# A transformer tower on one core: softmax remainders by pairs of units, one rounded exponential less in every sixth pair, value products two steps later

## The reference

```
nb = s // w                                  # 8 blocks of 128 queries
sb = einsum('bhnqd,bhnkd->bhnqk', qb, kb)    # each block sees 3 blocks of keys
probs = softmax(concatenate([sg, sb + bias])) # sg: the score of the global token 0
out = einsum('bhnqk,bhnkd->bhnqd', pb, vb) + einsum('bhsg,bhgd->bhsd', pg, vg)
out = out.at[:, :, g].set(og)                # token 0 attends to everything
```

## Time and profile before

| | |
|---|---|
| median of the runs | 921.63 us |
| profiled execution, its own time | 924.96 us |
| its span, first to last instruction | 923.2 us |
| mean granted TensorE clock | 0.954 of full speed |
| PE, PE weight loads | 805.3 us (87%), 615.1 us (67%) |
| DVE, ACT, POOL busy | 587.9 us, 583.4 us, 555.3 us |
| attention steps, round 1 | about 62 to 155 us of the span |

### The profile page before, as it was taken

How to read it: one execution, slowest core, us unless ns; L and a number is a source line. 1 busy time by engine, 2 the same in 40 slices (tenths; PEclk the granted TensorE clock), 3 DMA queues, 4 the chain that set the end, 5 groups by cost and what they waited for, 6 DMA issues and landing times.

```text
span 923.2 us, 23664 instructions
## 1 busy us (share of the span) xinstructions
PE 805.3 (87%) x8467; PEld 615.1 (67%) x8467; DVE 587.9 (64%) x1897; ACT 583.4 (63%) x1622; POOL 555.3 (60%) x820
## 2 busy tenths in 40 slices
PE   4989998999999989999999899999998977886397
PEld 1767766666777666667776666677765645785397
DVE  3678845447988454568884543798845436898454
ACT  2769985338799853277998534779985213665164
POOL 3548875544478755365887554448875445658345
PEclk9899999999999989999999999999998995999599
DMA  2320000602000006030000060200000613001231
GB/s 64 100 52 3 3 14 10 195 1 81 3 3 4 16 31 195 5 99 18 3 4 14 10 196 0 81 3 4 3 3 1 195 55 151 1 8 47 87 102 34
DMA packets 38597, 43.85 MB, mean 47 GB/s; under 512 B 7163, under 2 KB 33882, under 8 KB 38346
## 3 DMA queue, kind: packets, MB, share of 16 engines
q1 hardware_dynamic: 18348, 19.40, 7.1%
q10 hardware_dynamic: 17860, 18.19, 6.3%
q0 software_dynamic: 2272, 4.74, 1.6%
HBM read 20.70 MB, written 21.59 MB: 46 GB/s over the span
## 4 chain that ended last, share of the span: by engine, by line
PE 60%; DVE 13%; ACT 9%; issue 5%; SPq 5%; POOL 4%; DMA 2%; ACTq 1%; POOLq 0%; DVEq 0%
PE bank L1344 7%; PE bank L1481 6%; PE bank L1505 5%; PE bank L1432 4%; PE bank L1550 4%; PE bank L1551 4%; PE bank L1484 3%; PE bank L1370 3%; ACT p L732 3%; PE bank L1381 3%; PE bank L1435 3%; PE bank L1651 2%; PE bank L1660 2%; SPq L453 2%; DVE p L993 2%
## 5 line engine op out<-in xcount | busy, mean ns | idle before, releaser
L568 POOL TENSOR_TENSOR p<-p 128x384 f16<-128x384 f32 (+1 forms) x320 | 270.8, 859 | 110.2 <-ACT p L732 102.0
L986 DVE TENSOR_REDUCE nmx<-bank 128x1 f32<-128x384 f32 (+1 forms) x384 | 191.0, 512 | 36.4 <-PE bank L1435 32.1
L731 ACT ACTIVATE p<-bank 128x384 f32<-128x384 f32 (+1 forms) x384 | 174.0, 453 | 42.6 <-PE bank L1484 28.9
L732 ACT ACTIVATE p<-bank 128x384 f16<-128x384 f32 (+1 forms) x384 | 174.0, 453 | 0.0
L1481 PE MATMUL bank<-stack 103*128 103x128 bf16 x1056 | 145.1, 222 | 4.4 <-DMA stack<-mtr 3.1
L1484 PE MATMUL bank<-bandb,idb 128*128 128x128 bf16 x672 | 135.3, 222 | 0.0
L1432 PE MATMUL bank<-stack 100*128 100x384 bf16 (+1 forms) x384 | 120.3, 313 | 1.6 <-DVE nmx L986 1.3
L1505 PE MATMUL bank<-vst,p 128*128 128x49 bf16 x2112 | 115.5, 185 | 1.7 <-POOL p L568 1.7
L1481 PEld LDWEIGHTS bank<-stack 103*128 103x128 bf16 x1056 | 88.2, 98 | 28.9 <-issue 15.6
L1435 PE MATMUL bank<-bandb,idb 128*128 128x128 bf16 x672 | 100.9, 219 | 0.0
L1505 PEld LDWEIGHTS bank<-vst,p 128*128 128x128 f16 x2112 | 91.7, 97 | 11.6 <-POOL p L568 2.1
(11 more groups left out here) (252 smaller groups left out, 1799.7 us busy)
## 6 DMA issues: line engine op xcount, KB each, us to landing
xs<-zrow ACTq DMA_DIRECT2D x8, 2193.0 KB, 11.8
xt<-xs SPq DMA_DIRECT2D x23, 129.0 KB, 2.1
w2s<-in_w SPq DMA_DIRECT2D x4, 576.0 KB
mwbs<-in_mwb SPq DMA_DIRECT2D x1, 2064.0 KB, 9.1
mw2s<-in_mw SPq DMA_DIRECT2D x1, 2048.0 KB, 13.4
lnrow<-in_lnr SPq DMA_DIRECT2D x4, 480.0 KB
stack<-mtr SPq DMA_DIRECT2D x96, 3.0 KB
w1b<-in_w SPq DMA_DIRECT2D x4, 291.0 KB
```

The lines of the kernel that those rows point to most:

```text
L568: nc.gpsimd.tensor_tensor(p2[:, u % RING, 0:w], p32[:, u % RING, 0:w], p1[:, u % RING, 0:w], ALU.subtract).then_inc(p2_pool, 1)
L731: nc.scalar.activation(p32[:, s % RING, 0:w], ps[2 + s % 3][:, 0:w], ACT.Exp).then_inc(p32_ready, 1)
L732: nc.scalar.activation(p1[:, s % RING, 0:w], ps[2 + s % 3][:, 0:w], ACT.Exp).then_inc(p1_ready, 1)
L986: nc.vector.tensor_reduce(nmx[:, vn % 3, h:h + 1], nat_bank(v)[:, 0:w], AX.X, ALU.max, negate=True).then_inc(max_done, 1)
```

## The change

Five edits, all in the attention steps:

1. POOL forms remainders for two units in one instruction (128 x 768 at the inner blocks, 128 x 512 at the edge blocks), at every second step, once both units' exponentials are done.
2. In every sixth pair (units 10 and 11 of each 12) ACT writes only the 32-bit exponential. POOL rounds both units to 16 bits with one copy, and DVE forms the two remainders, one unit a step, at step u + 4 instead of u + 1.
3. `PV_LAG` goes from 4 to 6: value products, `combine` and the end of the loop come two steps later. The PE transposes of the output and ACT's copies of it stay at their steps.
4. `RING` goes from 6 to 10.
5. ACT's two copies of a block's output (lines 737, 738) stand ahead of that step's exponentials instead of behind them.

The diff, cut to its core:

```diff
-PV_LAG = 4
+PV_LAG = 6
-RING = 6
+RING = 10
@@ gpsimd @@
-                        u = s - 1
+                        p = s // 2 - 1
...
-                        if 0 <= u < U and u % SHARE != SHARE - 1:
-                            pool.wait_ge(p1_ready, at(p1_ready, u + 1))
-                            if u >= RING:
-                                pool.wait_ge(pv_mm, at(pv_mm, u - RING + 1))
-                            w = len(window(u // H)) * P
-                            nc.gpsimd.tensor_tensor(p2[:, u % RING, 0:w], p32[:, u % RING, 0:w], p1[:, u % RING, 0:w],
-                                                    ALU.subtract).then_inc(p2_pool, 1)
+                        if s % 2 == 0 and 0 <= p < U // 2:
+                            u = 2 * p
+                            pool.wait_ge(exp_done, at(exp_done, u + 2))
+                            if u >= RING:
+                                pool.wait_ge(pv_mm, at(pv_mm, u - RING + 2))
+                            two, w = slice(u % RING, u % RING + 2), len(window(u // H)) * P
+                            if p % SHARE == SHARE - 1:
+                                nc.gpsimd.tensor_copy(p1[:, two, 0:w], p32[:, two, 0:w]).then_inc(p1_cast, 1)
+                            else:
+                                nc.gpsimd.tensor_tensor(p2[:, two, 0:w], p32[:, two, 0:w], p1[:, two, 0:w],
+                                                        ALU.subtract).then_inc(p2_pool, 1)
@@ scalar: now behind the copies of lines 737 and 738 @@
-                            nc.scalar.activation(p32[:, s % RING, 0:w], ps[2 + s % 3][:, 0:w], ACT.Exp).then_inc(p32_ready, 1)
-                            nc.scalar.activation(p1[:, s % RING, 0:w], ps[2 + s % 3][:, 0:w], ACT.Exp).then_inc(p1_ready, 1)
+                            ins = nc.scalar.activation(p32[:, s % RING, 0:w], ps[2 + s % 3][:, 0:w], ACT.Exp)
+                            if s // 2 % SHARE != SHARE - 1:
+                                ins = nc.scalar.activation(p1[:, s % RING, 0:w], ps[2 + s % 3][:, 0:w], ACT.Exp)
+                            ins.then_inc(exp_done, 1)
@@ vector @@
-                        v, u = s + LEAD, s - 1
+                        v, u = s + LEAD, s - 4
-                        cn, cr = divmod(s - 10, H)
+                        cn, cr = divmod(s - PV_LAG - HH, H)
-                        if 0 <= u < U and u % SHARE == SHARE - 1:
-                            dve.wait_ge(p1_ready, at(p1_ready, u + 1))
+                        if 0 <= u < U and u // 2 % SHARE == SHARE - 1:
+                            dve.wait_ge(p1_cast, at(p1_cast, u // 2 // SHARE + 1))
@@ tensor @@
-                            if w % SHARE == SHARE - 1:
-                                pe.wait_ge(p2_dve, at(p2_dve, w // SHARE + 1))
+                            p = w // 2
+                            if p % SHARE == SHARE - 1:
+                                pe.wait_ge(p2_dve, at(p2_dve, 2 * (p // SHARE) + w % 2 + 1))
                             else:
-                                pe.wait_ge(p2_pool, at(p2_pool, w + 1 - w // SHARE))
+                                pe.wait_ge(p2_pool, at(p2_pool, p + 1 - p // SHARE))
@@ all engines @@
-                    for s in range(0, U + 18):
+                    for s in range(0, U + PV_LAG + 14):
```

More of the change, by code:

```diff
@@ L303, in program @@
         t_mm = sem("t_mm")
-        p32_ready = sem("p32_ready")
-        p1_ready = sem("p1_ready")
+        exp_done = sem("exp_done")
+        p1_cast = sem("p1_cast")
         p2_pool = sem("p2_pool")
@@ L376, in program @@
             (3 * NB, (tr_mm,)),
-            (U, (nat_mm, max_done, t_mm, p32_ready, p1_ready, pv_mm)),
-            (U - U // SHARE, (p2_pool,)),
+            (U, (nat_mm, max_done, t_mm, exp_done, pv_mm)),
+            (U // 2 // SHARE, (p1_cast,)),
+            (U // 2 - U // 2 // SHARE, (p2_pool,)),
             (U // SHARE, (p2_dve,)),
@@ L495, in _ @@
                     if l == L - 1 and b + 1 < B:
[L497 removed]
+                        sp.wait_ge(p2_pool, at(p2_pool, U // 2 - U // 2 // SHARE))
                         sp.wait_ge(p2_dve, at(p2_dve, U // SHARE))
@@ L739, in step @@
                                                      ps[5][0:DHI, 2 * P + t0:3 * P], ACT.Copy).then_inc(at_copied, 1)
+                        if 0 <= s < U:
+                            w = len(window(s // H)) * P
+                            act.wait_ge(t_mm, at(t_mm, s + 1))
+                            if s >= RING:
+                                act.wait_ge(pv_mm, at(pv_mm, s - RING + 1))
+                            ins = nc.scalar.activation(p32[:, s % RING, 0:w], ps[2 + s % 3][:, 0:w], ACT.Exp)
+                            if s // 2 % SHARE != SHARE - 1:
+                                ins = nc.scalar.activation(p1[:, s % RING, 0:w], ps[2 + s % 3][:, 0:w], ACT.Exp)
+                            ins.then_inc(exp_done, 1)
                     def evacuate(b, g):
@@ L1405, in step @@
                         if s == U + 4:
-                            pe.wait_ge(p1_ready, at(p1_ready, U))
+                            pe.wait_ge(exp_done, at(exp_done, U))
                             for i in range(3):
@@ L1477, in step @@
                             if s >= 3:
-                                pe.wait_ge(p1_ready, at(p1_ready, s - 2))
+                                pe.wait_ge(exp_done, at(exp_done, s - 2))
                             win = window(n)
```

5 lines of the change are left out of this document (removed).

## The result

The changed kernel takes 926.36 us (median of 13 runs, 924.19 to 930.12); the kernel before, run beside it, 923.06 us. The ratio is 1.0036, with a 95% interval of 1.002 to 1.0052: slower by 0.36%, small but told apart from no change. The profiled execution has a span of 928.2 us against 923.2.

What follows compares the result with a forecast made beforehand. PE was taken to bound the attention blocks (busy 10.57 of 11.10 us). Per round -0.2 - 5.3 + 4.5 + 1.35 + 0.7 = +1.05 us, over four rounds +4.2, so 921.6 + 4.2 = 925.8 us; 8-in-10 range 903 to 942.

Steps and rivals of the forecast that it cites:

- The waits that go and the turns that come: Attention blocks: PE's waits go, -5.3 us a round; DVE and POOL taking whole turns costs +4.5.
- The 0.9 us a block: Sixth pairs, five a round: PE stalls 0.54 us for DVE's second remainder and 0.37 for the row maximum behind it.
- the third row: PE's wait for DVE's third maximum row (line 1008), late behind a remainder: goes, 3.6 us a round.
- Durations from other forms: POOL instruction times inferred from other sizes: pair 1.59 us, edge pair 1.14, rounding copy of 768 columns 0.85.
- The seventh pair: Units 82 and 83, behind DVE's softmax of token 0: PE stands for about 1.35 us a round.
- both remainders wait: At units 82 and 83, DVE's two remainders wait for queued POOL pairs, 0.5 and 0.9 us.
- The softmax of token 0: End of step 84: ACT frees about 0.2 us earlier for it and PE waits less, -0.2 us a round.
- The end of the round: Last pair's copy and remainders and the sum for token 0, less earlier projections: +0.7 us a round (0.3 to 1.3).
- Elsewhere: Everything outside the attention stretches: the prediction's sum has no term for it, so 0.
- no turns: Rival, chance 0.28: DVE's remainder gets in while POOL works on a pair, so no stalls come; 902 to 906 us.
- POOL is first: Rival, chance 0.25 with a dear copy: POOL's pair starts before DVE's first remainder; 945 us if in all blocks, 935 in half.
- +6 a round more: Extra us a round if POOL's pair precedes DVE's first remainder: +1.4 a block in four or five blocks.

Runs made afterwards that it cites:

- e8: Changed kernel with the sum for token 0 moved behind the last value products; 928.55 us (one run).
- e1: Changed kernel, but DVE's instruction in its 64 units reads one SBUF tensor, leaving the subtraction out; 905.04 us, ratio 0.9774 to 0.9825.
- e3: Kernel before with only DVE's remainder of every sixth unit moved from step u + 1 to u + 2; 910.2 us, ratio 0.9826 to 0.9875.
- e4: Kernel before with DVE's remainder at step u + 2 and ACT's two output copies ahead of the exponentials; 901.06 us, ratio 0.9729 to 0.9778.
- e6: Changed kernel without the special sixth pair: ACT writes both exponentials everywhere, POOL forms all pairs; 908.22 us, ratio 0.9811 to 0.9851.
- e9: Changed kernel with DVE's remainders one step later, at u + 5 instead of u + 4; 977.6 us, ratio 1.053 to 1.062.
- e11: Changed kernel with a sixth pair's two DVE remainders back to back at step u + 4, behind an added tensor_scalar; 1011.05 us, ratio 1.0919 to 1.0995.
- e7: Changed kernel with two more DVE instructions of the same kind ahead of the first remainder of every sixth pair; 1029.43 us (one run).

## Why the prediction came out right, and where its steps did not

The forecast was 925.8 us, slower, from two large terms that nearly cancel. It stands on its central steps, and on errors that cancel too. By its own terms, per round:

- **The waits that go and the turns that come.** The two terms are -5.3 + 4.5 = -0.8 us up to unit 82. The trace has -0.2 / 4 = -0.05: -0.4, -0.1 and -0.4 in rounds 1 to 3, and +0.7 in round 0, where the first block came out long (e8, the same up to there, has 0.8 us less). The 0.9 us a block is 1.02 by e1. It was there for the reason given: first remainder 0.55, second 1.54 (1.46 forecast), PE's wait for it 10.7 us in all, 20 times. Of the 5.3 that goes, e3 and e4 measure the same thing from the side of before: 75.15 - 71.54 = 3.6 us of stream for the third row (3.6 forecast), 75.15 - 69.61 = 5.5 with the copies.
- **Durations from other forms.** Pair 1.64 (1.59 taken), edge pair 1.15 (1.14), rounding copy 0.82 and 0.61 (0.85 and 0.63), a pair behind a remainder about 2.0 (2.0). The copy took the value of the nearest row in kind; at the upper bound of 1.59, by the prediction's own walk, the order would have turned (not tried).
- **The seventh pair, +1.35: wrong.** The step "both remainders wait" failed. DVE went first both times, and the stretch from unit 82 to 94 fell by 1.2 / 4 = 0.3 us a round (single rounds spread there from 12.9 to 14.6 us, with the clock). The turns were assumed fair at a place where they are not, for a reason that stays open.
- **The softmax of token 0, -0.2: not seen.** Its last instruction on DVE (line 953, now 960) starts 3.25 us behind the exponential of unit 83 and not 3.11, so later and not earlier, and PE's wait for it grew by 0.4 us a round. In e6, where ACT and POOL treat this pair like the others, it is 1.9 us again. In the kernel before, over the four rounds:

```profile
PE bank L1388 <- DVE hid L953: 7.7, 4, 1.9
```

- **The end of the round, +0.7: 0.95 us measured**, within the bound of 1.3. ACT's copies ahead of the last exponentials (0.31) were missing from it.
- **Elsewhere, 0: about +0.65.** This is a mean of uneven parts: 0.4 us ahead of the first round's attention, 0.9 behind round 0, -0.1 and 0.0 behind rounds 1 and 2, 1.5 behind the last. The stretch from the first projection of round 0 to the next attention took 90.94 instead of 90.04 us, with PE's clock at a mean 0.96 instead of 1.00:

```profile
155.57:245.61 90.04, 82.61 (x558) 59.38 (x558) 57.51 (x175) 47.66 (x103) 39.83 (x81) 1.00 0.23 72
```

```profile
158.71:249.65 90.94, 84.47 (x554) 61.81 (x555) 57.44 (x175) 47.39 (x100) 39.73 (x81) 0.96 0.24 71
```

  The end of the round is longer by the same 0.95 us in all four rounds, and the part behind the last round is 0.7 us shorter in e8 than in the kernel before, so this does not follow the change in any way that the traces show. It may be spread between executions.

The errors add to 0.75 (what goes and what comes) - 1.45 (the seventh pair and token 0) + 0.25 (the end) + 0.65 (elsewhere) = +0.2 us a round: the main mechanism was right, but that the time came within 1 us is luck. (The medians differ by 3.3 us, the two profiled executions by 5.0; the rest is the spread between executions.) Of the rivals, "no turns" (0.28) is ruled out by every block of the trace; its 902 to 906 us is nevertheless what the kernel would take, since e1, where the turns can't happen, came at 905. "POOL is first" did not happen, but by 0.05 us: e9 and e11 show it 51 and 85 us above the changed kernel. The range to 942 us was too narrow on that side for the chance that it had. Two sums of the prediction don't come out as written. The bounds that it states for its terms give +0.35 to +2.65 us a round, 923 to 932 us, and not -1.0 to +3.0. And "+6 a round more" is 24 us, so "POOL is first" by its own terms was 950 us in all and 938 in half, and not 945 and 935.

## What to carry to other kernels

Two engines that take turns at one resource are priced by how often one asks while the other is in a long instruction, not by busy time: the same bytes in one instruction instead of two took 17 us less, a form with one SBUF input (which left the subtraction out) 21 us less. Pairing took POOL's instruction from 0.91 to 1.64 us, and with it what one short instruction of DVE can lose. And before work is regrouped to get rid of a wait, see what stands directly ahead of the late instruction: here one step in one line, and the order of two statements, gave some 23 us (924.3 to 901.1), where the regrouping lost 3.

## What the runs showed of the hardware that was not expected

- The turns alternate: whoever waits goes next, even against an engine that has its next instruction ready (e7: DVE 0.55, 2.0, 2.0 us in a row; POOL's two pairs 3.91 together). The Trainium skill, SBUF — State Buffer, "Who interferes with whom", calls the ports that the two share an exclusive lock and says that the order of issue decides who blocks; the inner blocks here agree, with waits of up to 1.45 us (2.0 instead of 0.55 in e7). How the order goes on when both wait showed only in the runs, and not as one rule: at units 82 and 83 POOL's pair was issued 0.46 us ahead of DVE's first remainder, and yet DVE went twice, and in e7 four times, running.
- Some 0.15 us of start-up is hidden in such a wait, both ways, also with instructions of 1.64 us: POOL's pair ends 1.50 us behind the remainder that it waited for, and a remainder of 0.55 us ends 0.42 us behind the pair.
- Stalls of PE cost more than their own length where the clock falls with them: against 10.19 us without any, blocks of e9 with two stalls take 12.1 to 12.4 us where the granted clock stayed at 1.00 and 15.28 us where it came to 0.78.
